# A graph network's edge sweep: VectorE's pair comparison in two halves, and its comparisons set between other work

## What is computed

```python
# L0, for edge e with source row x = h[src], destination row y = h[dst]
msg   = einsum('eb,ebo->eo', w_comp[etype], einsum('ei,bio->ebo', x, weight))   # 16 bases
x_hat = x @ A1_w.T + A1_b
y_hat = y @ A2_w.T + A2_b + rel_emb[etype]
a     = tanh(relu(sum(x_hat * y_hat) / sqrt(32)))
nei   = segment_sum(a[:, None] * msg, dst)
h_new = relu(where(in_deg > 0, nei + h[src[last edge of dst]] @ self_loop_weight, 0))
# L1: segment_sum(x[src], dst);  L2: softmax attention over each node's edges;
# L3: ten steps of normalised propagation over the same edges
```

## Time and profile before

| | |
|---|---|
| median of 3 runs | 1178.94 us (1175.4 to 1184.0) |
| the profiled execution | 1179.21 us |
| its span | 1177.4 us |
| mean granted TensorE clock | 0.866 |
| PE busy | 896.5 us (76%) |
| VectorE busy | 929.4 us (79%) |
| ScalarE busy | 507.7 us (43%) |
| POOL busy | 640.4 us (54%), 638.5 us of it the 568 gathers |

### The profile page before, as it was taken

One profiled execution on the slowest core, in us unless ns is written; L12 is line 12 of the kernel. 1 busy time (PEld: TensorE's weight loads), 2 busy tenths in 40 slices (PEclk: granted clock), 3 DMA queues, 4 the chain that ended last, 5 costly groups with the idle time before them and its releaser, 6 DMA issues.

```text
span 1177.4 us, 55398 instructions
## 1 busy us (share of the span) xinstructions
PE 896.5 (76%) x23682; PEld 846.3 (72%) x23682; DVE 929.4 (79%) x1684; ACT 507.7 (43%) x1244; POOL 640.4 (54%) x580
## 2 busy tenths in 40 slices
PE   3358887868688768776787777767376968999996
PEld 2357877767587667776776677766376968999996
DVE  8869999978798879887888787887647996555556
ACT  0235655444554447664756566656458410000000
POOL 5777777777777777777777787877000000000000
PEclk9568999987798889888878888889587989999998
DMA  4432322322233223222322223231000000000001
GB/s 114 60 72 55 63 59 54 64 55 45 51 56 55 53 45 60 49 53 50 60 47 54 49 55 62 44 55 29 4 3 2 4 3 4 4 5 4 4 5 18
DMA packets 54911, 47.93 MB, mean 41 GB/s; under 512 B 35966, under 2 KB 45182, under 8 KB 54662
## 3 DMA queue, kind: packets, MB, share of 16 engines
q0 software_dynamic: 18176, 9.34, 9.7%
q1 hardware_dynamic: 30822, 14.16, 5.8%
q10 hardware_dynamic: 5664, 20.84, 4.8%
HBM read 41.98 MB, written 2.31 MB: 38 GB/s over the span
## 4 chain that ended last, share of the span: by engine, by line
POOL 42%; PE 23%; DVE 16%; issue 15%; DMA 2%; ACT 2%; DVEq 0%; ACTq 0%; SPq 0%
POOL arena L633 42%; PE ps L885 13%; PE ps L932 3%; DVE arena L1373 2%; PE ps L916 2%; PE ps L856 2%; PE ps L895 2%; DVE aggT L1417 1%; DMA arena<-line_table 1%; ACT arena L1122 1%; DVE arena L1368 1%; DVE arena L1404 1%; DMA arena<-rel_rows_in 1%; DVE arena L1388 1%; PE ps L818 0%
## 5 line engine op out<-in xcount | busy, mean ns | idle before, releaser
L633 POOL DMA_INDIRECT arena<-x_pad,arena x568 | 638.5, 1124 | 173.4 <-issue 173.1
L818 PE MATMUL ps<-aggT 128*128 128x128 f16 x3024 | 230.1, 247 | 44.3 <-DVE aggT L1417 44.3
L818 PEld LDWEIGHTS ps<-aggT 128*128 128x128 f16 x3024 | 216.5, 114 | 49.0 <-DVE aggT L1417 49.0
L1404 DVE TENSOR_TENSOR arena<-ps,arena 128x1536 f32<-128x1536 f32 x98 | 172.4, 1759 | 3.4
L885 PE MATMUL ps<-arena,adj_words 128*128 128x64 f16 x5625 | 171.9, 192 | 3.3 <-DVEq L1666 3.2
L885 PEld LDWEIGHTS ps<-arena,adj_words 128*128 128x128 fp8e4 x5625 | 170.5, 97 | 4.6 <-DVEq L1666 3.5
L1075 ACT ACTIVATE adj_words<-arena 128x500 uint8 x196 | 126.5, 645 | 56.6 <-ACT arena L1050 54.9
L780 PE MATMUL ps<-arena 128*32 128x44 f32 (+4 forms) x7048 | 134.5, 215 | 20.2 <-DVE arena L1404 20.0
L1045 ACT ACTIVATE arena<-ps 128x500 fp8e4<-128x500 f32 x196 | 113.0, 577 | 79.0 <-PE ps L767 79.0
L780 PEld LDWEIGHTS ps<-arena 128*32 128x32 f32 x7048 | 110.5, 115 | 43.8 <-DVE arena L1404 26.7
L1373 DVE TENSOR_TENSOR arena<-pair_no,arena 128x2400 bf16<-128x2400 f16 x98 | 137.3, 1401 | 0.0
(11 more groups left out here) (222 smaller groups left out, 1153.2 us busy)
## 6 DMA issues: line engine op xcount, KB each, us to landing
arena<-line_table ACTq DMA_DIRECT2D x48, 344.0 KB
arena<-x_pad,arena POOLq DMA_INDIRECT x568
arena<-pick_table SPq DMA_DIRECT2D x27, 256.0 KB
arena<-line_table ACTq DMA_DIRECT2D x48, 80.0 KB
arena<-dst_parts SPq DMA_DIRECT2D x196, 5.7 KB
agg_table<-arena SPq DMA_DIRECT2D x196, 2.5 KB
dst_parts<-aggT SPq DMA_DIRECT2D x1, 735.0 KB
x<-x_pad SPq DMA_DIRECT2D x1, 400.0 KB
```

Of the source, the lines that this page charges most:

```text
L633: pool.indirect_dma_start(to, None, table, bass.IndirectOffsetOnAxis(ap=index, axis=0)).then_inc(done, 16)
L818: mm = nc.tensor.matmul(ps[:, at:at + PICK_WIDE * FEAT], pick_hot[:, u % PICK_RING, k * P:(k + 1) * P], x_parts[:, t, j * PICK_WIDE:(j + 1 ...
L1404: v.tensor_tensor(mixed[:, d % 2, :, :, 0:BASES], fetched_of(d)[:, :, SCORED:REL_COLS].unsqueeze(2).to_broadcast(n), weighted.unsqueeze(3) ...
```

## The change

In the sweep, on VectorE alone:
- `make_pairs` loses the rows comparison, which becomes `make_rows` and now comes last and raises `pairs_ready`. The pair comparison becomes two tensor-tensor instructions of 4 slots (1200 elements per partition) each instead of one of 8 (2400). The wait for `pairs_used` stands before the first half.
- `score_edges` becomes `products_of` and `scores_of`; the first half of the pair comparison stands between them, so that the wait for the product's completion comes after it.
- On duos that read picked rows, the second half stands between the masking product and the sum of halves, and the rows comparison between the two sums.
- `make_mixed` becomes `make_last`, `weigh` and `make_mixed`; of the pick comparisons one comes before `make_last`, the others between `weigh` and the mixed product.
- `make_lines` (L1352) moves from behind the pair comparison to the end of the duo, behind the mixed product; `make_dst_hot` stands behind the rows comparison.

Nothing changes in what is computed, nor on the other engines or in any DMA. The core of the diff:

```diff
-                def make_pairs(d):
-                    h = d % 2
-                    if d >= 2:
-                        dve.wait_ge(pairs_used, (d - 1) * DUO)
+                def make_rows(d):
                     n = [P, WIDE, P // 2, 2]
-                    v.tensor_tensor(row_hot[:, h].rearrange("p k (v i) -> p k v i", i=2),
+                    v.tensor_tensor(row_hot[:, d % 2].rearrange("p k (v i) -> p k v i", i=2),
...
+                def make_pairs(d, k0, k1):
+                    if k0 == 0 and d >= 2:
+                        dve.wait_ge(pairs_used, (d - 1) * DUO)
+                    n = [P, k1 - k0, HOTS * BLOCKS // 2, 2]
+                    v.tensor_tensor(pair_hot[:, d % 2, k0:k1].rearrange("p k (v i) -> p k v i", i=2),
...
-                    link(v.tensor_tensor(product, fetched_of(d)[:, :, 0:SCORED], xp[:, d % AHEAD], ALU.mult))
+                    step(v.tensor_tensor(product, fetched_of(d)[:, :, 0:SCORED], xp[:, d % AHEAD], ALU.mult))
+
+                def scores_of(d):
+                    chain.wait()
                     v.tensor_reduce(score[:, d % 2, :], product, AX.X, ALU.add).then_inc(score_ready, 1)
...
                 for d in range(DUOS):
-                    score_edges(d)
-                    if d + 1 < DUOS:
-                        make_pairs(d + 1)
-                    c = d // LINE_DUOS
+                    c, own = d // LINE_DUOS, UNITS_AT.get(d, [])
+                    picked_now, more = PICK_READ_AT.get(d), d + 1 < DUOS
+                    products_of(d)
+                    if more:
+                        make_pairs(d + 1, 0, SLOTS)
+                    scores_of(d)
+                    if picked_now is not None:
+                        mask_picked(picked_now)
+                    if more:
+                        make_pairs(d + 1, SLOTS, WIDE)
+                    if picked_now is not None:
+                        add_halves()
+                    if more:
+                        make_rows(d + 1)
+                    if picked_now is not None:
+                        add_pairs(picked_now)
+                    if d % LINE_DUOS == 1 and c + 1 < LINES:
+                        make_dst_hot(c + 1)
+                    for n in own[0:1]:
+                        make_pick_hot(*n)
+                    make_last(d)
+                    weigh(d)
+                    for n in own[1:]:
+                        make_pick_hot(*n)
+                    make_mixed(d)
                     if d % LINE_DUOS == 0 and c >= 1 and c + 1 < LINES:
                         make_lines(c + 1)
-                    if d % LINE_DUOS == 1 and c + 1 < LINES:
-                        make_dst_hot(c + 1)
-                    if d in PICK_READ_AT:
-                        read_picked(PICK_READ_AT[d])
-                    for c, j in UNITS_AT.get(d, []):
-                        make_pick_hot(c, j)
-                    make_mixed(d)
```

More of the change, by code:

```diff
@@ L1380, in fetched_of, with products_of @@
                     return ps[:, at:at + WIDE * REL_COLS].rearrange("p (k c) -> p k c", k=WIDE)
-                def score_edges(d):
+                def products_of(d):
                     dve.wait_ge(fetched, d + 1)
@@ L1387, in score_edges, with make_last @@
                         dve.wait_ge(gathered[d % AHEAD], 16 * tiles)
[L1388 removed]
+                    step(v.tensor_tensor(product, fetched_of(d)[:, :, 0:SCORED], xp[:, d % AHEAD], ALU.mult))
+                def scores_of(d):
+                    chain.wait()
                     v.tensor_reduce(score[:, d % 2, :], product, AX.X, ALU.add).then_inc(score_ready, 1)
[L1391 to L1393 removed]
+                def make_last(d):
                     if d >= 2:
@@ L1399, in make_mixed, with weigh @@
                                     ALU.is_equal)
+                def weigh(d):
+                    at = d % LINE_DUOS * WIDE
                     dve.wait_ge(weight_ready, d + 1)
-                    link(v.scalar_tensor_tensor(out=weighted, in0=weight_e[:, d % 2, :].unsqueeze(2).to_broadcast(n),
-                                                scalar=0.0, in1=own_hot, op0=ALU.max, op1=ALU.mult))
+                    step(v.scalar_tensor_tensor(out=weighted,
+                                                in0=weight_e[:, d % 2, :].unsqueeze(2).to_broadcast([P, WIDE, HOTS]), scalar=0.0,
+                                                in1=dst_hot[:, d // LINE_DUOS % 2, at:at + WIDE, :], op0=ALU.max, op1=ALU.mult))
+                def make_mixed(d):
+                    chain.wait()
                     n = [P, WIDE, HOTS, BASES]
@@ L1418, in make_pick_hot, with mask_picked @@
                      .then_inc(pick_hots, 1)
-                def read_picked(c):
+                picked_of = picked.rearrange("p (k w f) -> p k w f", k=WIDE, w=PICK_WIDE)
+                def mask_picked(c):
                     dve.wait_ge(pick_used, PICK_DEEP * (c + 1))
                     n = [P, WIDE * PICK_WIDE, FEAT]
-                    link(v.tensor_tensor(picked.rearrange("p (w f) -> p w f", f=FEAT),
+                    step(v.tensor_tensor(picked.rearrange("p (w f) -> p w f", f=FEAT),
                                          ps[:, PICK_AT_BANK:PICK_AT_BANK + WIDE * PICK_WIDE * FEAT]
@@ L1426, in read_picked, with add_halves @@
                                          pick_mask[:, c].rearrange("p k w -> p (k w)").unsqueeze(2).to_broadcast(n), ALU.mult))
+                def add_halves():
+                    half = PICK_WIDE // 2
+                    chain.wait()
                     dve.sem_inc(pick_read, 1)
-                    of = picked.rearrange("p (k w f) -> p k w f", k=WIDE, w=PICK_WIDE)
-                    half = PICK_WIDE // 2
-                    link(v.tensor_tensor(of[:, :, 0:half], of[:, :, 0:half], of[:, :, half:PICK_WIDE], ALU.add))
@@ L1431, in read_picked, with add_pairs @@
-                    link(v.tensor_tensor(xp[:, PICKED[c] % AHEAD, :, 0:FEAT], of[:, :, 0, :], of[:, :, 1, :], ALU.add))
+                    step(v.tensor_tensor(picked_of[:, :, 0:half], picked_of[:, :, 0:half], picked_of[:, :, half:PICK_WIDE], ALU.add))
+                def add_pairs(c):
+                    chain.wait()
+                    step(v.tensor_tensor(xp[:, PICKED[c] % AHEAD, :, 0:FEAT], picked_of[:, :, 0, :], picked_of[:, :, 1, :], ALU.add))
                 make_lines(0)
                 make_dst_hot(0)
-                make_pairs(0)
+                make_pairs(0, 0, WIDE)
@@ L1436, in run_sweep @@
+                make_rows(0)
                 make_lines(1)
                 for d in range(DUOS):
-                    score_edges(d)
-                    if d + 1 < DUOS:
-                        make_pairs(d + 1)
-                    c = d // LINE_DUOS
+                    c, own = d // LINE_DUOS, UNITS_AT.get(d, [])
[23 more added lines that the diff above has]
+                    make_mixed(d)
```

8 lines of the change are left out of this document (3 added, 5 removed).

## The result

| | before | after |
|---|---|---|
| median | 1181.86 us (7 runs, 1175.4 to 1184.0) | 1171.23 us (7 runs, 1168.24 to 1175.23) |
| ratio to before | | 0.9922, 95% interval 0.9896 to 0.9947 |
| profiled execution, its span | 1179.21, 1177.4 us | 1169.64, 1167.8 us |
| POOL in the 568 gathers | 638.5 us | 628.6 us |
| VectorE busy | 929.4 us | 913.4 us |

The kernel is 0.8% faster, some 9 us on the ratio, where 16 us had been forecast. The profiled executions differ by 9.6 us and POOL's time in gathers by 9.9 us.

What follows compares the result with a forecast made beforehand. POOL's 568 back-to-back gathers were taken to bound the sweep, with 94.5 us of excess. Averaged phases left 68 us (26 less), locked ones 87 (7 less); the middle, -16, gave 1179 - 16 = 1163 us, range 1146 to 1184.

Steps and rivals of the forecast that it cites:

- What bounds the kernel, and what moves it: Sweep: POOL's 568 gathers one behind another bound it; their 94.5 us of excess are what the change can move.
- The rule that two inputs in SBUF hold a gather's start: VectorE's L1368 and L1373: a gather starting during such an operation of length D is held for D - 0.13 us.
- I take the middle, -16 us: Last step of the sum: between 26 us less (phases averaged) and 7 us less (phases locked), giving 1163 us.
- a single pick at a gather's end: One L1417 (0.48 us) in the new order: costs 0.05 us at a gather's start and hardly reaches its end.
- phases averaged: Loss averaged over where in the gather's cycle VectorE's comparisons begin: 68 us of excess, 26 less than before.
- phases locked: Plain duos followed without VectorE waits, phases repeating: 1.04 us per duo, 87 us of excess, 7 less than before.
- The follower that meets the rows: Plain duo: the gather after one let go by the first half, due at 1.885, loses 0.39 us in the rows comparison.
- L1352 in the open: Line comparison at the end of even duos, no longer behind L1373: costs 0.22 us every other duo, 0.11 per duo.
- VectorE's part: VectorE's own work shrinks by some 0.15 us per duo, 15 us in all, which buys nothing itself.
- No change: Rival: phases lock, or gathers' landings set VectorE's steps; 1170 to 1182 us, say 1175; chance 0.23.
- Slower: Rival: uncovered L1352 costs each of 47 gathers up to 0.62 us, 29 us, second L1417 25 us; chance 0.12.
- Twice the gain: Rival: halves and rows are met in gaps, only single holds remain, about 0.5 us per duo; 1134 us; chance 0.15.

Runs made afterwards that it cites:

- psum_lines: Kernel before with the slots' numbers of both comparisons copied to PSUM and L1352 at the end of the duo: 1101.69 us, ratio 0.9323.
- psum_before: Kernel before with only the slots' numbers of both comparisons copied to PSUM once per duo: 1131.88 us, ratio 0.9595.
- together: Kernel after with the first half of the pair comparison moved behind the scores' sum: 1145.92 us, ratio 0.9711.
- split_lines: Kernel before with the pair comparison as two halves back to back and L1352 at the end of the duo: 1141.02 us, ratio 0.9639.
- whole_after: Kernel after with the pair comparison whole again, in the place of the second half: 1181.56 us, ratio 1.0003.

## Why the prediction was right in kind and wrong in size

**What bounds the kernel, and what moves it:** right. POOL's gap-free chain, its mean falling with the time, and the excess over 0.945 us as the amount at stake (94.5 us before; 20.5 us are left in psum_lines) were borne out by every kernel of the table. L633's mean was forecast at 1.096 us and came to 1.107; gathers of 2.4 us or more fell from 20 to 1, and those of 1.3 to 1.8 us rose from 40 to 124, the way it was said.

**The rule that two inputs in SBUF hold a gather's start:** right; psum_before shows it with nothing else changed but one small copy per duo. It goes against what the Trainium skill, SBUF — State Buffer, section "Who interferes with whom", infers: that descriptor generation needs the write interface of the shared pair, of which a tensor-tensor takes only the read one. The prediction left out that the same section has an instruction with two SBUF inputs contend with a GpSimd instruction that reads SBUF. A gather reads its row numbers from SBUF (`src_t`), and the holds at its start (409.35 in the earlier trace rows, 1.43 us for 0.94) agree with that sentence. By the inference the comparisons' part would have stayed and the tensor-scalars' fallen. In fact the comparisons' fell by 8.2 us (61.5 to 53.3) and the tensor-scalars' by 5.2 (32.1 to 26.9).

**The step that failed** is the last one of the sum, "I take the middle, -16 us", and with it the price of a single pick at a gather's end. The two ends were 68 us of excess (phases averaged) and 87 us (phases locked); the middle is 77.5. Measured were 85.1 us after 57 us (83.4 by the windows), near the locked end. By parts, in us:

| | averaged | locked | measured |
|---|---|---|---|
| comparisons, with L1430's sum | 46 | 62 | 57.2 |
| tensor-scalars | 22 | 25 | 26.9 |

The averaged row is (71 x 0.51 + 27 x 0.46) x 0.95 and (71 x 0.25 + 27 x 0.20) x 0.95; the locked one puts 0.745 and 0.295 for the 0.51 and 0.25. I had argued that VectorE's 25 waits break the lock. They break it in part: two thirds of the odd duos sit in the locked place (0.17 us reckoned, 0.16 to 0.17 found), half of the even ones near it (0.42 reckoned, 0.44 to 0.49 found), and a plain duo loses 0.62 us at the comparisons, where 0.51 and 0.745 had been reckoned. The comparisons thus cost 3 us more than the middle, and the tensor-scalars 3.4 us more, above both ends. Taking the locked sum alone, -7 us, would have been within 4 us of the result, but in part by luck: it has the comparisons 5 us too high and the tensor-scalars 2 too low.

**Terms inside it.** The follower that meets the rows was seen in advance (0.39 to 0.40 us on two of three duos), yet it went into an average; together shows that it was the main thing to see in this order. L1352 in the open was priced at 0.11 per duo, 11 us; measured 12.4. A single pick at a gather's end was taken at 0.08 us on odd duos in the locked sum, and at next to nothing in the averaged one; the gather of 409.24, let go at 409.75, should have ended at 410.56, is caught by L1426 (ends 410.54) and ends at 410.84, 0.06 us after the two-input L1399 behind it: 0.28 us. Thirty gathers end like that, 8.3 us in all, of which the locked sum had some 2.7. Why they end 0.30 us after the pick is open: the end lies just behind L1399, but five other gathers of this kernel and fourteen of the kernel before are caught by a pick with the same short comparison right behind it, and end 0.12 us after the pick.

**VectorE's part:** right that it costs and brings nothing. The halves took 773 ns (774 forecast) and VectorE's work fell by 16 us (15 forecast). The tanh came later and L1406 waited 26.2 us for it (6.6 us for L1401 before), a wait that I had priced at zero by its cover; it was covered, as the 78.4 us before L1389 show.

**The rivals.** "No change" by a lock was the nearer one in mechanism and the result lies between it and the forecast. "Slower", by L1352 in the open, had the mechanism (12.4 us) but not the price (29). "Twice the gain" (1134 us) would have needed phases in the gaps; together and split_lines came near its time (1146 and 1141 us) by another order, not by better phases in this one.

## What to carry to other kernels

When an engine works without a gap, look at the spread of one instruction's duration: its mean over its undisturbed time, times its count, is what other engines take from it, and the chain of waits will never name them. Before instructions are cut or moved apart to let another engine in, follow where its next start falls: two short holds at the distance of its period were worse here than the same two in a row (25 us). An average over phases needs a reason that the phases mix; where both loops are regular, follow one period by hand and expect the result nearer to that. And a hold that depends on where an operand lies is better removed than scheduled around: here halving and placing brought anything from nothing (whole_after) through 10 us (the change) to 43 (split_lines), and the operand's move another 33 to 71 us in whatever order it was tried.

## What the hardware showed that I had not expected

- A two-input comparison with one input in PSUM runs at the speed of the one with both in SBUF (16-bit data, 1200 elements in 771 ns against 773, 2400 in 1398 against 1401, 1024 in 682 against 684) and holds no gather.
- An indirect gather can be held at two places. At its start two-input operations in SBUF and tensor-scalars hold it, and once let go it needs 0.81 us. At its end only tensor-scalars were seen to catch it, and it mostly ends 0.12 us after them; thirty gathers of the kernel after took 0.30 us there.
- 60 us more work on an engine with slack made the kernel 7 us faster.
